# Order of the leftover value products and the next group's third scores on TensorE

## The reference

```
x = x + layernorm(attention_block(layernorm(x)))
x = x + layernorm(moe(layernorm(x)))

attention_block(x):                      # 16 heads of width 8, causal
    xn = rms_norm(x, ln1_w)
    q, k, v = xn @ Wq, xn @ Wk, xn @ Wv  # q and k normalised per head
    p = softmax(mask((q.k + rel_bias[bucket(position difference)]) * scale))
    y = (p @ v) @ Wo + x
    return relu(rms_norm(y, ln2_w) @ W1) @ W2 + y      # W1: 128 x 512

moe(x):                                  # 8 experts of inner width 352, the top 2 per token
    w, e = top_2(softmax(x @ router_w.T))
    return sum over the 2 experts of w * (silu(x @ gate[e].T) * (x @ up[e].T)) @ down[e].T
```

## Time and profile before

| what | us |
|---|---|
| median of 3 runs | 591.67 |
| lowest and highest run | 591.47, 597.71 |
| the profiled execution: span from first to last instruction | 596.4 |
| TensorE matmul busy in it | 532.1 (89%) |
| ScalarE busy | 395.4 (66%) |
| VectorE busy | 375.9 (63%) |
| GpSimd busy | 349.7 (59%) |

### The profile page before, as it was taken

One profiled execution on the slowest core, in us unless ns is written; L12 is line 12 of the kernel. 1 busy time (PEld: TensorE's weight loads), 2 busy tenths in 40 slices (PEclk: granted clock), 3 DMA queues, 4 the chain that ended last, 5 costly groups with the idle time before them and its releaser, 6 DMA issues.

```text
span 596.4 us, 14609 instructions
## 1 busy us (share of the span) xinstructions
PE 532.1 (89%) x4952; PEld 395.0 (66%) x4969; DVE 375.9 (63%) x1095; ACT 395.4 (66%) x880; POOL 349.7 (59%) x449
## 2 busy tenths in 40 slices
PE   6989899899899899988899899999976899999981
PEld 5655455556566455655555666889976899999960
DVE  6824583965975947996847877527742365555347
ACT  3388989888978788869788696644531355555425
POOL 6104636545538885357877258487578555565545
PEclk9999999999999999999999999999996799999997
DMA  7245333213213322232734512212122203321174
GB/s 196 76 126 161 111 99 109 74 37 108 80 45 122 102 86 71 77 100 78 201 109 134 132 56 52 59 55 69 55 61 69 55 32 86 88 63 32 33 287 141
DMA packets 47016, 55.62 MB, mean 93 GB/s; under 512 B 7376, under 2 KB 41056, under 8 KB 44784
## 3 DMA queue, kind: packets, MB, share of 16 engines
q1 hardware_dynamic: 42624, 45.76, 26.7%
q0 software_dynamic: 4320, 8.92, 4.5%
HBM read 36.27 MB, written 18.92 MB: 93 GB/s over the span
## 4 chain that ended last, share of the span: by engine, by line
PE 56%; DVE 15%; ACT 10%; POOL 6%; issue 6%; DMA 3%; another core or an unknown queue 3%; DVEq 1%; SPq 0%; ACTq 0%; POOLq 0%
PE SC L871 11%; PE OA L748 9%; PE OA L881 6%; PE M L786 4%; PE M L822 4%; PE SC L730 3%; ACT arena L1015 3%; PE SC L734 2%; PE M L643 2%; DVE SS L1330 2%; PE SC L740 2%; PE M L662 1%; POOL slots L1782 1%; PE M L852 1%
## 5 line engine op out<-in xcount | busy, mean ns | idle before, releaser
L1015 ACT ACTIVATE arena<-SC 128x1024 f32<-128x1024 f32 x160 | 161.9, 1039 | 14.7 <-PE SC L735 11.8
L871 PE MATMUL SC<-arena 128*128 128x128 f32 (+1 forms) x852 | 111.5, 283 | 0.0
L871 PEld LDWEIGHTS SC<-arena 128*128 128x128 f32 (+1 forms) x852 | 104.0, 191 | 0.4 <-issue 0.3
L748 PE MATMUL OA<-arena 128*32 128x256 f32 (+1 forms) x1536 | 88.9, 349 | 6.6 <-DVE arena L455 2.8
L1782 POOL DMA_INDIRECT slots<-XBA,IDX x64 | 72.6, 1134 | 37.0 <-DVE IDX L1455 19.6
L1503 DVE TENSOR_TENSOR arena<-arena,SC 128x256 f32<-128x256 f32 (+1 forms) x142 | 43.7, 348 | 68.6 <-issue 24.6
L881 PE MATMUL OA<-arena 128*128 (+1 forms) x426 | 62.5, 284 | 12.9 <-issue 8.1
L748 PEld LDWEIGHTS OA<-arena 128*32 128x32 f32 x1536 | 39.2, 109 | 44.0 <-issue 22.8
L881 PEld LDWEIGHTS OA<-arena 128*128 128x128 f32 (+1 forms) x426 | 55.2, 198 | 15.4 <-issue 15.4
L454 POOL TENSOR_TENSOR arena<-arena 128x512 f32<-128x512 f32 x32 | 42.7, 1335 | 36.2 <-ACT arena L1015 35.6
L447 POOL TENSOR_TENSOR arena<-arena 128x512 f32<-128x512 f32 x23 | 31.2, 1356 | 48.9 <-ACT arena L1015 48.8
(11 more groups left out here) (244 smaller groups left out, 1086.0 us busy)
## 6 DMA issues: line engine op xcount, KB each, us to landing
arena<-parts SPq DMA_DIRECT2D x90, 192.0 KB
parts<-arena SPq DMA_DIRECT2D x16, 384.0 KB
arena<-ytok SPq DMA_DIRECT2D x8, 512.0 KB, 7.3
XGA<-slots SPq DMA_DIRECT2D x39, 65.0 KB
arena<-slots SPq DMA_DIRECT2D x32, 65.0 KB, 1.9
X<-in_L_attn_x SPq DMA_DIRECT2D x4, 512.0 KB, 5.1
out<-X SPq DMA_DIRECT2D x8, 256.0 KB, 2.5
arena<-parts SPq DMA_DIRECT2D x12, 96.0 KB
```

The source lines that it names most:

```text
L748: mm = pe.matmul(OA[32 * j:32 * j + 32, q0:q0 + n], vals[:, t, 32 * h:32 * h + 32], probs(j), start=first, stop=last, skip_group_check=True)
L871: mm = pe.matmul(SC[0:n, r % 2, 512 * m + P * c:512 * m + P * (c + 1)], WSEL[s % 4][:, I * m + i0:I * m + i0 + n], XGT[r % 2], start=True, ...
L1015: act.activation(EB[u], SC[:, n % 2, :], ACT.Exp).then_inc(exp_done, 1)
```

## The change

`pv23` of the group before stood behind the second unit's scores, and ahead of the other work of that position; `pv4` stood behind the third unit's scores. Now both stand ahead of the third unit's scores, and so behind all other work of the second unit's position. Batch 0 has no leftovers in its first group. At the first position behind batch 7 both were already issued together, and are so still.

```diff
--- before.py
+++ after.py
@@ -949,6 +949,10 @@
                 at = PE_AT[b >= NB]
                 for n in positions(b):
                     g, u = divmod(n, UNITS)
+                    before = (b, g - 1) if g else (b - 1, GROUPS - 1)
+                    if b < NB and u == 2 and before[0] >= 0:
+                        pv23(*before)
+                        pv4(*before)
                     if b < NB:
                         scores(b, n)
                     if b == 0 and n in TABLE_AT:
@@ -959,12 +963,9 @@
                             table_rows(k, i)
                     if b == NB and n == 0:
                         early(0)
-                    before = (b, g - 1) if g else (b - 1, GROUPS - 1)
-                    if 0 <= before[0] < NB and (b < NB or before[0] == NB - 1 and b == NB and g == 0):
-                        if u == 1 and b < NB or n == 0 and b == NB:
-                            pv23(*before)
-                        if u == 2 and b < NB or n == 0 and b == NB:
-                            pv4(*before)
+                    if b == NB and n == 0:
+                        pv23(*before)
+                        pv4(*before)
                     if b < NB and u == 4:
                         pv01(b, g)
                     if 1 <= due(PRE["val"], b, n) < NB:
```

## The result

| | kernel before | changed kernel |
|---|---|---|
| median of 4 runs, us | 593.57 | 610.25 |
| lowest and highest | 591.47, 597.71 | 608.51, 615.43 |
| span of the profiled execution | 596.4 | 609.1 |
| start of the last exponential of batch 7 | 367.0 | 381.5 |

The ratio is 1.030 (95% interval 1.023 to 1.036): slower. The forecast was 590.8, within 586 to 596, with 0.11 on slower. All of the loss in the profiled execution comes up to the last exponential of the attention stage (14.5 us there); behind it the changed kernel is 1.8 us shorter (227.6 against 229.4). On the other chips of the experiments the same kernel gave 1.011 and 1.012 where the kernel before takes 580 us, and 1.023 where it takes 594.

The account below looks back on a forecast made before the run. TensorE sets the pace (busy 37.4 of 40 us), with little room over ScalarE and VectorE. Crossing 1 +1.16, crossing 2 -0.85, crossing 3 -1.21, crossing 0 0: -0.90 on the median 591.67 gives 590.8 us, range 586 to 596.

Parts of the forecast that it names:

- crossing 1: Leftover value products at units 6 and 7: exponential +0.57, first hidden product +0.33 us; +1.16 in all, with count.
- crossing 2: Leftover value products at units 11 and 12: -1.15 us over batches 0, 1, 2, 4, 6, +0.3 in batch 7; -0.85.
- count: Unit 6, batch 3: both products behind `count`, TensorE idle about 1.0 us, exponential +1.33, hidden product +1.0; 0.7 left.
- crossing 3: Units 16 and 17: query and key projection earlier, gain passing ScalarE, TensorE and VectorE's norm sums alike; -1.21 us in all.
- the joining: Each crossing: value products in one piece save 0.13 us, scores 0.10, so 0.23 us less TensorE time.
- the cover that I named: Batch 5: the count wait is covered, since `pv23` of crossing 2 already stands 1.10 us for VectorE's slowed multiply.
- Rival 2: Late third scores never made good: crossing 1 0.33, crossing 2 0.44 each, count 1.0 more thrice; +7.9, 599.6 us; chance 0.11.
- crossing 0: Units 1 and 2, last group of the batch before: `out_bank` released up to 0.54 us earlier, but covered; 0.
- Rival 1: Every crossing pays in full: 31 x 0.23 us plus 2.95 at crossing 3, less 1.85; -8.2, 583.5 us; chance 0.12.
- XART's 0.59: Crossing 3, batches 0 to 4: the projection must wait for ScalarE's XART, so 0.59 of 1.01 us is won.
- batch 6's 0.75: Crossing 3, batch 6: both products behind a weight transpose's wait, later exponential delays POOL's product and next batch's root; +0.75 us.
- batch 7's 0.4: Crossing 3, batch 7: last exponentials wait for the third scores, and the next phase for the last one; +0.4 us.

Follow-up runs that it names:

- h_fill4: Changed kernel plus useless identity matmuls in TensorE's waits for the norm, the count and the fifth unit's product (unit 2, batches 4, 6), on a 580 us chip; 1.006.
- e_fill: Changed kernel plus useless identity matmuls in TensorE's waits ahead of the norm's transposes (batches 3, 4, 6) and of the count (batches 3, 5); ratio 1.011.
- e_cross3: Kernel before with only the query and key projection moved ahead of `pv23` at unit 16 of batches 0 to 5; ratio 1.003.
- e_split: Changed kernel with `pv4` put back behind the third unit's scores, so nothing joined; `pv23` stays behind the second unit's other work; ratio 1.027.
- e_pool: Changed kernel with one wait added: GpSimd's multiply at unit 3 of batches 0 to 6 waits for the next batch's norm; ratio 1.011.
- i_fill4: The same program as h_fill4, run on a 594 us chip; ratio 1.023 to the kernel before.
- f_before: The kernel before, unedited, run and profiled again on a 594 us chip; ratio 1.001, median 593.89 us.

## Why the prediction was wrong

h_fill4 has the order of the change and the full clock, so its exponentials show the order's own price. It ran on kind A, and the kernel before's profile is of kind B; but e_fill has the same steps within 0.03 but for batch 6, and the first profile of the change, on kind B, has them in batches 0, 1 and 7, where nothing else disturbs it. The start of unit 2, against the kernel before, from batch to batch (the last row up to the last exponential):

| batch | forecast | measured in h_fill4 | what differs |
|---|---|---|---|
| 0 | -1.02 | -0.65 | crossing 1 costs 0.24, crossing 2 costs 0.13; 0.40 gained at unit 2 |
| 1 | -0.49 | -0.48 | crossing 1 costs 0.51, not 0.33; 0.18 gained at unit 2 |
| 2 | -0.49 | +1.50 | norm: +1.93 at unit 5 |
| 3 | +0.70 | +2.70 | norm: +1.93 at unit 5; count +1.88 at unit 7 |
| 4 | -0.82 | -1.36 | more of crossing 1 regained |
| 5 | 0 | +1.30 | norm: +1.93; count +1.87, of which 1.17 is back at unit 12; crossing 3 -1.05 |
| 6 | +0.52 | +0.09 | |
| 7 | +0.70 | +0.56 | |
| sum | -0.90 | +3.66 | |

1. **The step that failed first** is in crossing 3: "VectorE's norm sums behind it have about as much idle ahead". I let the gain of 0.59 per crossing run through all engines alike. ScalarE's exponential of unit 3 came 1.25 us earlier and VectorE 0.41, and that difference pushed GpSimd's multiply into the norm. Three times 1.93 us is 5.8, more than the whole sum; taken off, the sum is -2.1 us, the forecast's own sign. That is a subtraction and not a run: where the norm was repaired, the count wait grew. That this belongs to the step and not to the joining is shown by e_cross3 (2.51 us for the norm) and e_split (3.04), that it is GpSimd, by e_pool (1.43). Both operations overlap in the trace of before, by 0.11 us and without harm, and I didn't look at them, since the change does not touch them.
2. **The count** was mis-sized. The wait is as long as forecast (1.14 against 1.0), but the exponential of unit 7 steps by 1.88 and not 1.33, and in batch 3 only 0.25 of it came back behind it, at unit 8. In batch 5 the cover that I named, the wait for the multiply at unit 12, gave back 1.17 as written.
3. **The clock** had no term, and it is the largest part. From 100 us on the kernel before keeps 2.4 GHz with idle times of up to 1.35 us (the prediction read 1.09 as its longest; 1.35 stands at unit 18 of batch 5, at 278.74); the change makes some of 1.6 to 2.6. The profiled execution loses 14.5 us up to the last exponential: 3.7 of the order (h_fill4), 2.4 of ScalarE's wait in batch 4, and 8.4 that remain for 21 us at half clock. That fits the price seen singly: a single short stretch at half clock cost 1.45 to 1.6 us, three times in i_fill4 and once in f_before. Two profiles of the changed kernel on chips of kind A lose 11.1 and 5.6 in all at 0.96 and 0.98. Rows of 4 us at 0.51 to 0.58 right behind the idle times, and none where these were filled, show the cause; how much of the median it is, is only bounded, since run for run the clock falls at different ones of these idle times.
4. **The size on chips of kind B** stays open in part. The change cost 1.1% and 1.2% on two chips of kind A, 2.3% and 3.0% on two of kind B. ScalarE's wait at unit 7 is part of it, seen in three profiles, all with the order of the change; its cause isn't known, and filling idle times didn't help there.

Rival 2 (599.6) had the right side, and its reason holds in part. In h_fill4 the third exponential is 0.75 to 0.85 later at crossing 1 of batches 1 and 2, and 0.5 to 0.6 of it stays up to unit 11, more than its 0.33; but at crossing 2 the exponential is 0.43 later and 0.42 of that is back at the next unit, so that half of its sum is not there, and batch 1 as a whole comes out at the forecast, by luck in part: what crossing 1 costs beyond its 0.33 is gained at the next unit 2, in crossing 0, which I had put at 0. Rival 1 fails too: the joining's 0.23 is real, but it stays only where nothing else waits. The joining, XART's 0.59 and batch 6's 0.75 were sized right; of batch 7's 0.4 half was left (0.21). The prediction's own mark against it, the phase behind the attention stage changed by more than 0.5 us, came true (-1.8). The clock is 0.96 there against 0.94 in the kernel before, which is the likely reason; no run separates it.

The chances were too sure: every term was taken from waits that the trace of before shows, and none for waits that only a shift of 0.4 to 1.2 us between engines would bring about.

## What to carry to other kernels

When a change moves one engine's work earlier by a microsecond and another's by less, list the pairs of VectorE and GpSimd operations that pass each other closely, and price each as VectorE standing still until GpSimd's operation ends. Before putting an operation that waits for a late engine ahead of the work that feeds ScalarE, add up TensorE's new idle time: here even 0.8 to 1.6 us of it could cost another 1.5 through the clock. And a repair that takes one wait away is worth only the distance to the next wait on the same late engine; two of them here only moved the idle time to TensorE's next wait for VectorE, and no gain shows in the medians.

## What the runs showed of the hardware

- Four VectorE multiplies of 128 x 256 in float32 with both inputs in SBUF took 1.43 us alone, 2.51 when GpSimd's multiply of 128 x 512 started 0.67 in, and 3.04 when it started 0.44 in and one of 128 x 256 behind it ran into them too; each VectorE multiply that was held up ended 0.28 us behind GpSimd's. GpSimd's own first multiply went from 1.28 to 1.57 and 1.46.
- Two changes between scores and value products cost 0.13 us (32 passes in one piece 1.44 to 1.51, apart 0.57 and 1.01) and 0.10 (scores 0.54 or 0.44).
- TensorE's clock fell to 1.2 GHz behind single idle times of 0.79 to 2.8 us, in some executions and not in others of the same kernel at the same idle time (0.57 and 1.00 behind 1.59 us), and behind none of 23 that were filled with useless matmuls. A single short stretch at 1.2 GHz cost 1.45 to 1.6 us, four times.
- Chips differ: 580 or 594 us for the same kernel; the stretch behind the last exponential took 211 to 215 or 220 to 229 us.
